# One attention and feed-forward layer on one core: projections, attention and feed-forward as three phases, key tiles in a new order over eight banks

## The chip, the core and the metric

The kernel runs on one core of one Trainium2 chip (trn2). The metric is the device time of one execution in microseconds (us), the median of several runs. "Before" is the kernel as it stands, "after" the changed one.

## What is computed

The input x has 4 batches of 512 tokens with 512 features, all in float32. Attention has 32 query heads of width 16 in 8 groups; each group of four query heads shares one key head and one value head. Then follows a layer norm of x plus the result, a sparse feed-forward step (in each block of 32 of its 1792 inner features one is kept, the one where a low-rank guess is largest), and a layer norm again.

```python
x = L0_attn_x
x = _layernorm(x + _L0_attn_ref(x, L0_attn_wq, L0_attn_wk, L0_attn_wv, L0_attn_wo), axis=-1)
x = _layernorm(x + _L0_ffn_ref(x, L0_ffn_c1_w, L0_ffn_c2_w, L0_ffn_w1, L0_ffn_w2t), axis=-1)
# attention, for every batch b and group g of NKV = 8:
scores = jnp.einsum('bqgrd,bkgd->bgrqk', qg, k) / jnp.sqrt(jnp.asarray(HD, x.dtype))
attn = jax.nn.softmax(scores.astype(jnp.float32), axis=-1).astype(x.dtype)
out = jnp.einsum('bgrqk,bkgd->bqgrd', attn, v)
```

## The kernel before

Where float32 accuracy is wanted from the faster matmul type, a tensor is held as a high part and a low part (`_h`, `_l`), and a product is three matmuls: high by high, high by low, low by high. A **unit** is one batch and one group: four query heads by 512 queries by 512 keys. There are NU = 32 units, in order of batch. A **key tile** is a quarter of a unit: 128 keys against all 4 x 512 queries.

*Projections.* `project(b, s)` (12 matmuls, L645) makes 128 rows of q, k or v of a batch; there are TASKS = 6 of them per batch. ScalarE copies the high part out of PSUM, VectorE the low part, and SyncE (`store_projection`, L202) writes both to DRAM (`q_stacks`, `k_stacks`, `v_halves`), from where `load_unit` (four transfers, L218 and L219) and `load_v` read them back. Batches 0 to 2 are projected ahead of attention; the six tasks of batch 3 lie between key tiles of the first units (`LATE_AT`).

*Attention.* The operands of a unit lie twice in SBUF, in rows 0 to 49 and 64 to 113, so a matmul uses the upper (a = 0) or lower (a = 1) half of TensorE's rows. For a key tile TensorE does:
- four **scores** `scores_t(n, kt, r)` (L707), keys by queries, each into one bank of `ps_st` (two banks), which ScalarE turns into `probs` by one exponential each (L486);
- one **weighted sum** `weigh` (L721), four heads side by side in 32 columns each, eight matmul records;
- four **maxima matmuls** `scores(n + 2, ...)` (L670), queries by keys, for the unit after next, whose rows VectorE reduces to maxima (L509) two at a time.

The maxima of a unit are subtracted inside the score matmul, as two more rows of q (the **shift**). Its way: VectorE splits them into high and low (L516, L518), TensorE turns them (`turn_max`, L689, four matmuls into bank `ps_x`), ScalarE copies them (L446), and SyncE sends them to rows 48, 49, 112 and 113 of q (L233). `scores_t` of the first key tile of a unit waits for `shift_in`. Once in a unit ScalarE moves the sums out (`take_sums`, L452). The output projection of a batch (`project_out`, L737, four of 12 matmuls), its residual and its layer norm lie in units 5 and 6 of the next batch; before it the sums are read back (`load_sums`), multiplied with reciprocals (L412, GpSimd) that one transfer has spread over partitions (L259), and split (L458 ScalarE in the key tiles of `HIGH_AT`, L415 GpSimd).

*Feed-forward.* 4 x 14 slots (b, m); in each TensorE does 12 matmuls up (L1211), one for the marks (L1222), 12 down (L1234) and four small transposes (L1199), with preparing steps (`slot_steps`) in between. Batch 3's output projection is a step there (`wo`, L1171), batch 0's first transposes and its low-rank product were done in attention (`turn_x`, `first_u`).

The order on each engine is written out by hand: each engine runs its own loop, and semaphores tie them. PSUM in attention: four banks `ps_max`, two `ps_st`, one `ps_pv`, one `ps_x`.

## Time and profile before

| | us |
|---|---|
| median of 3 runs (lowest, highest) | 1001.59 (998.66, 1003.35) |
| the profiled execution, its own time | 998.58 |
| its span, first to last instruction | 996.8 |
| TensorE busy | 908.2 (91%) |
| VectorE busy | 562.4 (56%) |
| ScalarE busy | 442.9 (44%) |
| GpSimd busy | 193.1 (19%) |
| mean granted TensorE clock, share of full | 0.944 |

"Busy" is the time in which an engine has an instruction in flight. TensorE's instructions overlap one another, so its share says little of how much work it does in that time. A row of the timeline or of a group gives the engine, the line of the kernel, the operation, what it writes and reads, and in square brackets how long the engine had stood idle and for whom it waited. "PEclk" is the granted clock as a share of 2.4 GHz: 1.00 is 2.4 GHz, 0.50 is 1.2 GHz.

### The profile page before, as it was taken

Reading aid. Unit: us, or ns where it says so; the run is one execution under the profiler, and the core shown is the slowest. Engines: PE = TensorE matmul, PEld = TensorE weight load, DVE = VectorE, ACT = ScalarE, POOL = GpSimd, SP = SyncE. Lnnn points to the kernel's source line nnn. Section 1 sums busy time; section 2 is a strip of 40 time slices with the busy share of each in tenths; the row PEclk is TensorE's granted clock in tenths of the full one; section 3 lists DMA queues with packets and bytes.
Section 4 is the critical chain, followed back from the end, with each engine's and each line's share of the span. In section 5 each row is a group of like instructions: output and inputs, shape, how many; then the busy total and the mean of one; then the engine's idle time right before and its main releaser. Section 6 shows DMA issues by size and latency. Waiting matters only on the chain. (4 is left out here: it accounts for less than half of the span.)

```text
span 996.8 us, 12134 instructions
## 1 busy us (share of the span) xinstructions
PE 908.2 (91%) x4472; PEld 533.0 (53%) x4472; DVE 562.4 (56%) x743; ACT 442.9 (44%) x821; POOL 193.1 (19%) x183
## 2 busy tenths in 40 slices
PE   5868999999899998999989975999999999999995
PEld 3745543333334333343333434777777777777774
DVE  4636567888656885468866533545563365326413
ACT  3302466777654775456765542322222222222231
POOL 6302003730210002100021002333321222122221
PEclk8889999999989998599988978999999999999998
DMA  8466535643342243323433124214030002001101
GB/s 249 160 205 240 169 110 159 175 123 91 91 117 69 76 134 80 97 85 79 135 82 109 34 97 102 82 44 155 14 116 11 1 3 103 2 1 43 42 1 42
DMA packets 50858, 92.99 MB, mean 93 GB/s; under 512 B 5648, under 2 KB 13840, under 8 KB 50288
## 3 DMA queue, kind: packets, MB, share of 16 engines
q1 hardware_dynamic: 49312, 87.05, 29.3%
q0 software_dynamic: 1488, 5.16, 1.9%
q8 instruction: 36, 0.59, 0.2%
q14 instruction: 22, 0.18, 0.1%
HBM read 56.80 MB, written 34.87 MB: 92 GB/s over the span
## 5 line engine op out<-in xcount | busy, mean ns | idle before, releaser
L509 DVE TENSOR_REDUCE neg_max<-ps_max 128x2 f32<-128x1024 f32 x256 | 302.9, 1217 | 90.1 <-PE ps_max L670 89.7
L486 ACT ACTIVATE probs<-ps_st 128x512 f32<-128x512 f32 x496 | 270.2, 595 | 142.6 <-PE ps_st L707 139.7
L707 PE MATMUL ps_st<-q,k 50*128 50x512 f32 x496 | 181.9, 511 | 28.5 <-ACT probs L486 27.6
L707 PEld LDWEIGHTS ps_st<-q,k 50*128 50x128 f32 x496 | 71.9, 192 | 203.1 <-ACT probs L486 156.8
L670 PE MATMUL ps_max<-k,q 48*128 48x512 f32 x512 | 152.8, 452 | 14.0 <-DVE neg_max L509 9.2
L721 PE MATMUL ps_pv<-probs,v 128*32 128x512 f32 x1024 | 147.3, 649 | 5.9 <-ACT probs L486 2.3
L978 POOL TENSOR_TENSOR g_l<-picked,g_h 128x512 fp32r<-128x512 f32 x56 | 73.1, 1306 | 286.9 <-ACT g_h L1017 286.9
L1003 ACT ACTIVATE mask_t<-ps_t 128x512 bf16<-128x512 bf16 x56 | 33.4, 597 | 163.6 <-PE ps_t L1199 163.6
L1211 PE MATMUL ps_h<-xt_h,w_h 128*128 128x512 f32 x224 | 93.8, 419 | 8.0 <-ACT relu L1010 8.0
L1073 DVE TENSOR_REDUCE top<-ps_prep 128x14 f32<-128x448 f32 x62 | 38.6, 623 | 99.0 <-PE ps_prep L1188 98.8
L670 PEld LDWEIGHTS ps_max<-k,q 48*128 48x128 f32 x512 | 75.6, 199 | 28.9 <-DVE neg_max L509 13.5
L1090 DVE SCALAR_TENSOR_TENSOR picked<-ps_z,relu 128x512 f32<-128x512 f32 x56 | 38.7, 691 | 90.6 <-ACT relu L1010 90.6
L1211 PE MATMUL ps_h<-xt_h,w_l 128*128 128x512 f32 x224 | 88.8, 397 | 0.0
L1211 PE MATMUL ps_h<-xt_l,w_h 128*128 128x512 f32 x224 | 88.8, 397 | 0.0
L1010 ACT ACTIVATE relu<-ps_h 128x512 f32<-128x512 f32 x56 | 33.6, 599 | 102.2 <-PE ps_h L1211 102.2
L1234 PE MATMUL ps_out<-w_h,g_h 128*128 128x512 f32 x160 | 71.2, 445 | 0.0
L1234 PE MATMUL ps_out<-w_h,g_l 128*128 128x512 f32 x160 | 63.2, 395 | 0.0
L1234 PE MATMUL ps_out<-w_l,g_h 128*128 128x512 f32 x160 | 63.0, 394 | 0.0
L1211 PEld LDWEIGHTS ps_h<-xt_h,w_h 128*128 128x128 f32 x224 | 43.1, 192 | 15.5 <-ACT relu L1010 8.1
L412 POOL TENSOR_TENSOR att<-att,inv 128x512 f32<-128x512 f32 x12 | 14.8, 1270 | 172.4 <-DMA inv<-reciprocals 172.4
L1211 PEld LDWEIGHTS ps_h<-xt_h,w_l 128*128 128x128 f32 x224 | 42.7, 191 | 9.4
L1211 PEld LDWEIGHTS ps_h<-xt_l,w_h 128*128 128x128 f32 x224 | 43.2, 193 | 6.2
(159 smaller groups left out, 1141.2 us busy)
## 6 DMA issues: line engine op xcount, KB each, us to landing
q_stacks<-parts SPq DMA_DIRECT2D x48, 256.0 KB
q<-q_stacks SPq DMA_DIRECT2D x64, 192.0 KB, 3.6
sums<-stage SPq DMA_DIRECT2D x32, 256.0 KB, 3.4
k<-k_stacks SPq DMA_DIRECT2D x64, 96.0 KB, 3.1
x_raw<-xT SPq DMA_DIRECT2D x16, 256.0 KB, 8.5
yf<-after_attention SPq DMA_DIRECT2D x4, 1024.0 KB, 5.3
w_raw<-w POOLq DMA_DIRECT2D x16, 224.0 KB, 3.1
w_raw<-w SPq DMA_DIRECT2D x14, 256.0 KB, 2.9
```

The lines of the kernel that those rows point to most:

```text
L486: nc.scalar.activation(probs[kt % 2][:, r], score_bank(n, r), ACT.Exp, scale=float(HD) ** -0.5).then_inc(exp_done, 1)
L509: nc.vector.tensor_reduce(neg_max[n % 2][:, i // 2, :, i % 2], ps_max[i % 2][:], AX.X, ALU.max, negate=True).then_inc(max_red, 1)
L670: mm = nc.tensor.matmul(ps_max[i % 2][:, a], q[n % QR][64 * a:64 * a + STACK, j, t * P:(t + 1) * P], k_[n % QR][64 * a:64 * a + STACK, :], ...
L707: nc.tensor.matmul(score_bank(n, r), k_[n % QR][64 * a:64 * a + ROWS, kt * P:(kt + 1) * P], q[n % QR][64 * a:64 * a + ROWS, j, :], start=T ...
L721: last = nc.tensor.matmul(ps_pv[32 * r:32 * r + VW], v[f % 2][:, kt, g], probs[kt % 2][:, r], start=(kt == 0), stop=(kt == TT - 1))
L978: nc.gpsimd.tensor_tensor(g_l[m % 2][:], picked[m % 2][:], g_h[m % 2][:].bitcast(F32), ALU.subtract).then_inc(g_ready, 1)
L1003: nc.scalar.activation(mask_t[m % 2][:], ps_t[:], ACT.Copy).then_inc(mask_t_ready, 1)
L1010: nc.scalar.activation(act_r[m % 2][:], ps_h[:], ACT.Relu).then_inc(relu_ready, 1)
L1073: nc.vector.tensor_reduce(top[t % 2][:], src, AX.X, ALU.max).then_inc(prep_half, 1)
L1090: nc.vector.scalar_tensor_tensor(picked[m % 2][:], ps_z[:], 1.0, act_r[m % 2][:], ALU.is_equal, ALU.mult).then_inc(picked_ready, 1)
L1211: last = nc.tensor.matmul(ps_h[:], w[:, k, m * P:(m + 1) * P], xx[b % 2][:, k], start=(k == 0 and n == 0), stop=(k == KT - 1 and n == 2))
L1234: last = nc.tensor.matmul(ps_out[t][:], g[m % 2][:, t * P:(t + 1) * P], w2_tile(*w, m), start=(m == 0 and n == 0), stop=(m == MT - 1 and n ...
```

## The change

- **Three phases.** All 24 projection tasks run first, the last two batches with the maxima of units 0 and 1 between them. q and k of all batches stay in SBUF (`parts`, four buffers laid over memory that is used later), v too; nothing of them goes to DRAM. `load_unit` copies a unit from SBUF to SBUF in 12 transfers.
- **Attention alone.** No projection and no output projection lies between key tiles. Bank `ps_x` becomes a third bank of `ps_st`, so all eight banks serve attention. A score waits until the third last exponential is done, not the second last.
- **New order of a key tile**: one maxima matmul, three scores, the weighted sum of the tile before, a score, three maxima matmuls, so that the row halves alternate. `take_sums` moves on ScalarE ahead of the third exponential of a unit's first key tile.
- **The shift goes another way.** VectorE turns the maxima itself (`nc.vector.transpose`, L498), GpSimd's queue writes them to DRAM in four transfers (L291), waits for these, and reads them back into q in two (L297). GpSimd's other work (`load_raw`, `high_raw`, `low_raw`, `scale`, `low_att`, `split_w1`) stands behind these sends in its one queue.
- **A front of the feed-forward phase** does the output projections of all four batches (16 x 12 matmuls, now into the banks of `ps_out`), with residual and norm, and batch 0's preparing steps. Batch 0's sums are scaled and split during attention (units 11 to 14), those of batches 1 to 3 in the front: `load_att(b)` reads the sums and spreads the reciprocals, GpSimd multiplies, ScalarE and VectorE split.
- In the slots `relu` writes into `picked`, and `pick` works in place; w2 is loaded from slot to slot into a buffer of its own.

**TensorE, one key tile in the middle of a unit** (`ps_st` scores, `ps_max` maxima, `ps_pv` weighted sum; `exp_done` counts exponentials, `max_red` reductions). Before:

```order
L707 MATMUL ps_st<-q,k 128x512 [waits exp_done]
L670 MATMUL ps_max<-k,q 128x512 [waits max_red]
L707 MATMUL ps_st<-q,k 128x512 [waits exp_done]
L670 MATMUL ps_max<-k,q 128x512
L670 MATMUL ps_max<-k,q 128x512 [waits max_red]
L707 MATMUL ps_st<-q,k 128x512 [waits exp_done]
L670 MATMUL ps_max<-k,q 128x512
L707 MATMUL ps_st<-q,k 128x512 [waits exp_done]
L721 MATMUL ps_pv<-probs,v 32x512 [waits stage_ready,exp_done]
L721 MATMUL ps_pv<-probs,v 32x512 x3
```

After:

```order
L602 MATMUL ps_st<-q,k 128x512 [waits exp_done] x3
L616 MATMUL ps_pv<-probs,v 32x512 [waits exp_done]
L616 MATMUL ps_pv<-probs,v 32x512 x3
L602 MATMUL ps_st<-q,k 128x512 [waits exp_done]
L589 MATMUL ps_max<-k,q 128x512 [waits max_red]
L589 MATMUL ps_max<-k,q 128x512
L589 MATMUL ps_max<-k,q 128x512 [waits max_red]
L589 MATMUL ps_max<-k,q 128x512
```

Of the four scores two stood ahead of the weighted sum and two behind, each next to a maxima matmul; now three stand ahead of it and one behind, and the maxima follow in one run.

**GpSimd, units 3 to 5 of the changed kernel** (`maxima` is the DRAM buffer of the shift, `max_rows` the turned maxima; `max_turned` counts turned units, `max_out` landed writes). The change's rows from the second transfer of one shift into q to the next shift's:

```order
L291 DMA maxima<-max_rows 4x8x32 x3
L297 DMA q<-maxima 2x1024 [waits st_mm,max_out]
L297 DMA q<-maxima 2x1024
L321 TENSOR_TENSOR wo_l<-wo_raw,wo_h 128x2048 [waits pre]
L322 TENSOR_TENSOR c_l<-c_raw,c_h 128x320
L324 TENSOR_TENSOR c_s<-c_raw,c_s 16x1792 [waits pre]
L291 DMA maxima<-max_rows 4x8x32 [waits max_turned,pre]
L291 DMA maxima<-max_rows 4x8x32 x3
L297 DMA q<-maxima 2x1024 [waits st_mm,max_out]
```

The splitting of wo, c1 and c2 (L321, L322, L324) stands between two shifts; the next shift's transfers can't be issued until it is done.

The diff, cut to its core:

```diff
@@ -59,281 +56,204 @@
...
-        ps_st = [ps(f"ps_st{j}", [P, S]) for j in range(2)]
+        ps_st = [ps(f"ps_st{j}", [P, S]) for j in range(3)]
         ps_pv = ps("ps_pv", [P, S])
-        ps_x = ps("ps_x", [P, S])
...
             def load_unit(n):
 
-                j, b = n % QR, n // NKV
+                j, b, g = n % QR, n // NKV, n % NKV
                 if n >= QR:
-                    sp.wait_ge(pv_done, TT * (n - QR + 1))
+                    sp.wait_ge(st_mm, TILES * (n - QR + 1))
                 elif n == 0:
-                    sp.wait_ge(ones_set, 2 * QR + 1)
-                if n % NKV == 0:
-                    for i in range(3):
-                        sp.wait_ge(part_out[i], DMA * parts_out((b + 1) * (REP + 1), i))
-                q_src = qs[n * Q_UNIT:(n + 1) * Q_UNIT].rearrange("(a p w) -> a p w", a=2, p=STACK)
-                k_src = ks[n * K_UNIT:(n + 1) * K_UNIT].rearrange("(p t) -> p t", p=STACK)
+                    sp.wait_ge(ones_set, 2 * QR)
+                if g == 0:
+                    sp.wait_ge(low_out, (REP + 1) * (b + 1))
+                src = parts[b][HD * g:HD * (g + 1)].bitcast(F32)
                 for a in range(2):
-                    rows = slice(64 * a, 64 * a + STACK)
-                    sp.dma_start(k_[j][rows].bitcast(F32), k_src).then_inc(unit_in[j], DMA)
-                    sp.dma_start(q[j][rows].rearrange("p j t -> p (j t)").bitcast(F32), q_src[a]).then_inc(unit_in[j], DMA)
-
-            def send_shift(n):
-
-                sp.wait_ge(shift_ready, n + 1)
-                for a in range(2):
-                    sp.dma_start(q[n % QR][64 * a + SHIFT:64 * a + SHIFT + 2].bitcast(F32),
-                                 shift[n % 2][4 * a:4 * a + 4].bitcast(F32)
-                                 ).then_inc(shift_in[n % QR], DMA)
+                    for c in range(3):
+                        rows = slice(64 * a + HD * c, 64 * a + HD * (c + 1))
+                        sp.dma_start(k_[j][rows].bitcast(F32), src[:, 0, (0, 0, 1)[c]]).then_inc(unit_in[j], DMA)
+                        sp.dma_start(q[j][rows].bitcast(F32), src[:, 1 + a::2, (0, 1, 0)[c]]).then_inc(unit_in[j], DMA)
...
@@ -358,92 +278,129 @@
...
+            def send_shift(n):
+
+                to = maxima[n * TILES * 2 * P:(n + 1) * TILES * 2 * P]
+                pool.wait_ge(max_turned, n + 1)
+                dst = to.rearrange("(c t o x) -> o t c x", c=8, t=TT, o=4)
+                for o in range(4):
+                    pool.dma_start(dst[o], max_rows[32 * o:32 * (o + 1)]).then_inc(max_out, DMA)
+                pool.wait_ge(max_out, 4 * DMA * (n + 1))
+                src = to.rearrange("(a h w) -> a h w", a=2, h=2)
+                if n >= QR:
+                    pool.wait_ge(st_mm, TILES * (n - QR + 1))
+                for a in range(2):
+                    pool.dma_start(q[n % QR][64 * a + SHIFT:64 * a + SHIFT + 2].rearrange("p j t -> p (j t)").bitcast(F32),
+                                   src[a]).then_inc(shift_in[n % QR], DMA)
...
+            send_shift(0)
+            for n in range(NU):
+                if n + 1 < NU:
+                    send_shift(n + 1)
+                if n == 1:
+                    load_raw()
+                if n == 3:
+                    high_raw()
+                if n == 4:
+                    low_raw()
+                if n == 12:
+                    scale()
+                if n == 14:
+                    low_att()
+                for i in range(KT * NC):
+                    if 22 + i // 2 == n:
+                        split_w1(i)
...
@@ -451,199 +408,162 @@
...
             for n in range(NU):
-                b, g = n // NKV, n % NKV
                 for kt in range(TT):
                     for r in range(REP):
                         i = (n * TT + kt) * REP + r
-                        if r == 2 and not b and (g, kt) in LATE_AT[1:]:
-                            high_projection(NB - 1, LATE_AT.index((g, kt)))
+                        if r == 2 and kt == 0 and n:
+                            take_sums(n - 1)
+                        if r == 3 and (n, kt) in HIGH_AT:
+                            high_att(HIGH_AT[n, kt])
                         act.wait_ge(st_mm, i + 1)
                         if r == 0 and n * TT + kt >= 2:
                             act.wait_ge(pv_done, n * TT + kt - 1)
-                        nc.scalar.activation(probs[kt % 2][:, r], score_bank(n, r), ACT.Exp,
+                        nc.scalar.activation(probs[kt % 2][:, r], ps_st[i % 3][:], ACT.Exp,
                                              scale=float(HD) ** -0.5).then_inc(exp_done, 1)
-                        if b and r == 2 and (g, kt) in HIGH_AT:
-                            high_att(b - 1, HIGH_AT.index((g, kt)))
-                    if kt == 0:
-                        if n:
-                            take_sums(n - 1)
-                    if kt == 1 and n + 1 < NU:
-                        turn_shift(n + 1)
             take_sums(NU - 1)
...
+            def turn_max(n):
+                dve.wait_ge(max_split, n + 1)
+                if n:
+                    dve.wait_ge(max_out, 4 * DMA * n)
+                nc.vector.transpose(max_rows[:], max_parts[:].rearrange("p t a h j -> p (t a h j)").bitcast(F32)
+                                    ).then_inc(max_turned, 1)
...
+                for kt in range(TT):
+                    step = n * TT + kt
+                    for pair in range(2 * step + TILES, 2 * step + 2 + TILES):
+                        if pair < NT // 2:
+                            row_max(pair)
+                        if n + 1 < NU and kt < 2:
+                            (high_max, low_max, turn_max, lambda n: None)[2 * kt + pair % 2](n + 1)
+                    if kt == 1 and n in DEN_AT:
+                        invert(DEN_AT[n])
...
@@ -651,167 +571,88 @@
...
             def scores_t(n, kt, r):
 
                 i = (n * TT + kt) * REP + r
                 if kt == 0 and r == 0:
                     pe.wait_ge(shift_in[n % QR], 2 * DMA * (n // QR + 1))
-                if i < 2:
-                    pe.wait_ge(evacuated, FRONT - 2 + i)
-                elif n < NU - 2 or (n, kt) == (NU - 2, 0):
-                    pe.wait_ge(exp_done, i - 1)
-                    if r == 2 and n == NU - 2:
-                        pe.wait_ge(max_red, 8 * NU)
+                if i < 3:
+                    task_taken(pe, max(j for j in range(LAST) if j % 4 == i))
                 else:
-                    pe.wait_ge(exp_done, i - 3)
+                    pe.wait_ge(exp_done, i - 2)
                 a, j = r % 2, r // 2
-                nc.tensor.matmul(score_bank(n, r), k_[n % QR][64 * a:64 * a + ROWS, kt * P:(kt + 1) * P],
+                nc.tensor.matmul(ps_st[i % 3][:], k_[n % QR][64 * a:64 * a + ROWS, kt * P:(kt + 1) * P],
                                  q[n % QR][64 * a:64 * a + ROWS, j, :], start=True, stop=True).then_inc(st_mm, 1)
...
+            for o in range(TASKS):
+                project(0, o)
+            for b in range(1, NB):
+                for o in range(TASKS):
+                    project(b, o)
+                    if o == 0:
+                        turn_v(b - 1)
+                    for pair in pairs_at(b, o):
+                        scores(2 * pair)
+                        scores(2 * pair + 1)
+            turn_v(NB - 1)
+            scores(2 * TILES)
             for n in range(NU):
-                b, g = n // NKV, n % NKV
                 for kt in range(TT):
+                    step = n * TT + kt
+                    ahead = 4 * step + 2 * TILES + 1
+                    scores(ahead)
                     scores_t(n, kt, 0)
-                    if n == 0 and kt == 0:
-                        scores(2, 0, 0)
-                    scores(n + 2, 2 * kt, 1)
                     scores_t(n, kt, 1)
-                    if kt or n:
-                        weigh(*divmod(n * TT + kt - 1, TT))
-                    if not b and (g, kt - 1) == LATE_AT[0]:
-                        turn_v(NB - 1)
-                    if not b and (g, kt) in LATE_AT:
-                        pe.wait_ge(shift_ready, n + 1 + (kt > 1))
-                        project(NB - 1, LATE_AT.index((g, kt)))
-                    if b and (g, kt) in WO_AT and n < NU - 2:
-                        project_out(b - 1, WO_AT.index((g, kt)), n + 1 + (kt > 1))
                     scores_t(n, kt, 2)
-                    scores(n + 2, 2 * kt + 1, 0)
+                    if step:
+                        weigh(*divmod(step - 1, TT))
                     scores_t(n, kt, 3)
-                    scores(n + 2, 2 * kt + 1, 1)
-                    scores(*divmod(8 * (n + 2) + 2 * kt + 2, 8), 0)
-                    if n == NU - 2 and (g, kt) in WO_AT:
-                        project_out(b - 1, WO_AT.index((g, kt)), n + 1 + (kt > 1))
-                    if n == NU - 2:
-                        turn_x(kt)
-                    if (n, kt) == (NU - 1, 1):
-                        first_u()
-                    if kt == 1 and n + 1 < NU:
-                        turn_max(n + 1)
+                    scores(ahead + 1)
+                    scores(ahead + 2)
+                    scores(ahead + 3)
             weigh(NU - 1, TT - 1)
...
+            def load_att(b):
+
+                if b >= 2:
+                    sp.wait_ge(att_split, REP * (b - 1))
+                src = sums[b * NKV * SUMS:(b + 1) * NKV * SUMS].rearrange(
+                    "(g r h d t) -> r h g d t", r=REP, g=NKV, h=2, d=HD)
+                for r in range(REP):
+                    sp.dma_start(att[:, r], src[r, 0]).then_inc(att_in, DMA)
+                if b == NB - 1:
+                    sp.wait_ge(rden_out, DMA)
+                at = b * NH * S
+                sp.dma_start(inv[:].rearrange("p r t -> p (r t)"),
+                             rden[at:at + NH * S].rearrange("(g o t) -> g o t", g=NKV, o=1).broadcast_to(
+                                 [NKV, HD, REP * S])).then_inc(inv_in, DMA)
...
+            def scale(b):
+                pool.wait_ge(att_in, REP * DMA * b)
+                pool.wait_ge(inv_in, DMA * b)
+                for r in range(REP):
+                    nc.gpsimd.tensor_tensor(att[:, r], att[:, r], inv[:, r], ALU.mult).then_inc(att_scaled, 1)
+
             pool.wait_ge(half_set, 1)
             low_w2(0)
+            scale(1)
+            root(0)
+            scale(2)
+            root(1)
+            scale(3)
+            root(2)
+            root(3)
...
+                project_out(0, t)
+            project_out(1, 0)
+            project_out(1, 1)
+            front(0)
+            front(1)
+            project_out(1, 2)
+            front(2)
+            front(3)
+            project_out(1, 3)
+            front(U)
+            project_out(2, 0)
+            front(marks(0, 0))
+            front(marks(0, 1))
+            project_out(2, 1)
+            front(marks(0, 2))
+            front(marks(0, 3))
+            project_out(2, 2)
+            project_out(2, 3)
+            inner_up(0, 0, (0, 1, 2, 3))
             turn_mask(0, 0)
+            for t in range(TT):
+                project_out(3, t)
```

## Rows read from the trace of the kernel before

**Rows 1.** Stages: stretch, length, busy of PE PEld DVE ACT POOL, clock, DMA share, GB/s
```profile
0.00:103.53 103.53, 75.12 (x277) 54.35 (x277) 51.60 (x63) 24.73 (x42) 28.17 (x32) 0.87 0.66 213
103.53:592.93 489.40, 450.32 (x2377) 184.50 (x2376) 330.08 (x372) 312.62 (x593) 69.16 (x76) 0.93 0.38 104
592.93:617.50 24.57, 14.49 (x58) 10.43 (x59) 9.99 (x16) 4.52 (x9) 3.90 (x4) 0.85 0.49 134
617.50:983.20 365.70, 365.26 (x1750) 281.58 (x1750) 163.18 (x275) 101.03 (x178) 90.83 (x71) 0.99 0.13 42
```

**Rows 2.** Page, costliest groups: busy, mean ns of one, idle before, what ended it
```profile
L509 DVE TENSOR_REDUCE neg_max<-ps_max 128x2 f32<-128x1024 f32 x256 | 302.9, 1217 | 90.1 <-PE ps_max L670 89.7
```

**Rows 3.** Timeline of one steady key tile: start us, length us, engine, line
```profile
350.81 0.51 PE L707 MATMUL ps_st<-q,k 50*128 50x512 f32 x2
...
351.35 1.09 ACT L486 ACTIVATE probs<-ps_st 128x512 f32<-128x512 f32 x2 [0.83 <-PE ps_st L707]
...
352.49 0.49 PE L707 MATMUL ps_st<-q,k 50*128 50x512 f32 x1
...
352.91 1.07 PE L721 MATMUL ps_pv<-probs,v 128*32 128x512 f32 x8
...
353.90 0.50 PE L707 MATMUL ps_st<-q,k 50*128 50x512 f32 x2
```

**Rows 4.** Timeline of VectorE, maxima split in two units that follow each other
```profile
353.90 0.17 DVE L516 CAST max_parts<-neg_max 128x16 fp32r<-128x16 f32 x1
...
366.41 0.17 DVE L516 CAST max_parts<-neg_max 128x16 fp32r<-128x16 f32 x1
```

**Rows 5.** Busy time by stretch: a wait, half clock, full clock, half clock again
```profile
265.80:268.97 3.17, 0.00 (x1) 0.01 (x1) 1.46 (x2) 1.17 (x3) 2.47 (x3) 1.00 0.31 111
269.50:283.50 14.00, 13.67 (x49) 4.47 (x48) 6.12 (x7) 8.02 (x15) 6.16 (x6) 0.51 0.23 61
284.00:300.00 16.00, 15.14 (x83) 6.51 (x80) 11.31 (x14) 9.74 (x20) 0.35 (x1) 1.00 0.49 131
390.00:418.00 28.00, 27.43 (x94) 9.21 (x95) 12.38 (x14) 14.71 (x28) 7.77 (x7) 0.50 0.24 66
```

**Rows 6.** Timeline of TensorE at half clock, the weighted sums of two tiles
```profile
406.64 1.93 PE L721 MATMUL ps_pv<-probs,v 128*32 128x512 f32 x8
...
411.19 1.93 PE L721 MATMUL ps_pv<-probs,v 128*32 128x512 f32 x8
```

**Rows 7.** Line L395, transfers issued by GpSimd: ns of an issue, us to landing
```profile
L395 POOL DMA_DIRECT2D w_raw<-w x16: 543/556/570, 161.2 to 206.5; - x16
...
DMA to landing us min/median/max: 2.7/3.1/5.1
```

**Rows 8.** DMA issues: KB each, median us from issue to landing
```profile
reciprocals<-inv_den SPq DMA_DIRECT2D x3, 64.0 KB, 1.6
```

**Rows 9.** Line L218, loads of k issued by SyncE: ns of an issue, us to landing
```profile
L218 SPq DMA_DIRECT2D k<-k_stacks x64: 307/422/1384, 53.1 to 526.1; - x64
...
DMA to landing us min/median/max: 2.0/3.1/8.4
```

**Rows 10.** Groups of instructions of the whole run, by line
```profile
L412 POOL TENSOR_TENSOR att<-att,inv 128x512 f32<-128x512 f32 x12 | 14.8, 1270 | 172.4 <-DMA inv<-reciprocals 172.4
...
L375 POOL TENSOR_TENSOR wo_l<-wo_raw,wo_h 128x2048 fp32r<-128x2048 f32 x1 | 4.6, 4552 | 0.1
```

**Rows 11.** Timeline of TensorE: the first matmul of the run
```profile
6.05 0.76 PE L645 MATMUL ps_st<-x_h,w_h 128*128 128x512 f32 x1 [6.05 <-DVE x_l L501]
```

**Rows 12.** Chain that ended last, two steps of it: start us, length us, what
```profile
603.95 12.36 DMA w_raw<-w
...
636.66 2.73 PE ps_prep L1171 x12
```

**Rows 13.** Timeline: reciprocals of batch 0 spread, and who waits for them
```profile
253.62 0.65 SPq L259 DMA_DIRECT2D inv<-reciprocals  x1
...
266.50 2.49 POOL L412 TENSOR_TENSOR att<-att,inv 128x512 f32<-128x512 f32 x2 [54.91 <-DMA inv<-reciprocals]
```

1037 lines of the change are left out of this document (454 added, 583 removed).

## Prediction

> **What bounds the kernel now.** I read the stages first, since one average would mix limits. By the busy times per stretch [rows 1], attention takes 489.4 us of the 996.8 us span and TensorE is busy in 450 of them; the slots of the feed-forward phase take 365.7 us with TensorE busy throughout; projections take 103.5 us with 28 us of TensorE idle. Then the costliest groups: VectorE's reductions of maxima are 302.9 us and stand idle 90 us for TensorE [rows 2], so VectorE does not bound attention, yet it puts a floor of 2.4 us under a key tile (two reductions).
>
> Third, the timeline of a steady tile [rows 3]. Scores at 350.81, exponentials from 351.35 (0.54 later), two of them in 1.09 us, ending 352.44; the next score at 352.49 (0.05 later); the weighted sum at 352.91 (0.42); the scores behind it at 353.90 (0.99). A tile is 3.09 us, and a unit without other work 12.51 us, by VectorE's split in two units [rows 4]. The tile is a loop: a score waits for an exponential to free one of two banks, the exponential for a score. TensorE's own work is shorter: at half clock, where it is 98% busy [rows 5], two weighted sums are 4.55 us apart [rows 6], so 2.3 us at full clock.
>
> Fourth, the clock. After TensorE idled 3.2 us at 265.8 the granted clock stood at 0.51 (1.2 GHz) for the next 14 us and came back to 1.00 with nothing but key tiles and the turning of the maxima on TensorE; a later one stayed at 0.50 for the 28 us shown [rows 5]. At half clock a tile is 4.55 us.
>
> **The change part by part.**
>
> *Projections.* Six tasks come forward from attention. A task is 12 matmuls of 128x512, 2.73 us by a step of the same shape in the chain [rows 12]. 24 of them are 65.5; the 33 maxima matmuls between them, at 2.73 / 12 = 0.23 each, 7.5; the first matmul starts at 6.05 [rows 11]; I add 5 for half clock at the start and for one late weight load. No q or k goes to DRAM and back. Sum 84 us, against 103.5 for 18 tasks, whose idle time the readback made.
>
> *A key tile.* I follow the new order round. The last exponential of a tile frees the bank of the third score: 0.05 later it runs, 0.42 later the weighted sum, 0.99 later the fourth score, 0.54 later its exponential, which takes 0.55. That is 2.55 us, all terms from [rows 3]. TensorE's 2.3 us and VectorE's 2.4 stay just under it. A unit's first tile costs more, since `take_sums` (one copy on ScalarE, about an exponential's length) stands before the third exponential and waits for the weighted sum: 3.2 us. Unit: 3 x 2.55 + 3.2 = 10.85 us, against 12.51. If the new run of three maxima lost the overlap of row halves, eight matmuls at 0.23 and 0.99 would make the tile 2.83 and the unit 12.0; that is the bound above.
>
> *The shift.* Here the change adds a wait. VectorE turns the maxima in a unit's second tile, by my count 5.2 us after the unit's first score (3.2 for the first tile, a reduction of 1.2 by [rows 2], 0.8 for the turn). From there GpSimd issues four transfers, waits for landing, and issues two more; the next unit's first score waits for these. The trace has no such way through this queue. Nearest are GpSimd's loads: 0.556 us an issue, 2.7 to 5.1 to landing, median 3.1, but of 224 KB each [rows 7]. These here carry 8 KB in all. Small writes of SyncE land in 1.6 us [rows 8], its loads in 2.0 at least [rows 9]. I take three issues (1.7), 2.0 for the write, one issue (0.55), 2.2 for the read and 0.2 for semaphores: L = 6.6 us, since the size is nearer to the small transfers. Ends: 5.9 with the fastest landings, 8.6 with 3.1 twice. The unit is then 5.2 + 6.6 = 11.8 us, not 10.85, and TensorE idles 0.95 us in each; by the ends 11.1 and 13.8. The four turning matmuls and ScalarE's copy vanish, off this path. The Trainium skill, page "DMA: Bandwidth & Descriptors", section "Anatomy of one DMA", gives a transfer of GpSimd about 2 us fixed and little for bytes; by it L would be some 6.4, while the trace's own rows of that queue say 8.6.
>
> At unit 4 the splitting of wo and c stands ahead of a shift in the queue: 4.55 us for wo [rows 10] and some 5 for c by size. That makes one shift about 2 us late, an idle time of some 3 us, which in the trace is what lowers the clock [rows 5]. I price one fall: 14 us at 4.55 instead of 3.1 us a tile loses 14 x (1 - 3.1 / 4.55) = 4.5 us.
>
> *Attention in all:* 32 x 11.8 = 378, plus 2 for the late shift, 4.5 for the fall and 3 for the last weighted sum: 387 us, against 489.4.
>
> *The front.* What stood in attention's gaps now stands alone. Batches 1 to 3 go through one `att` buffer, in rounds: sums read (4), reciprocals spread, product on GpSimd, split (2). The spread takes 12.9 us from issue at 253.62 to the multiplication that waited for it [rows 13]; the product is 4 x 1.27 [rows 10]. A round is 24 us. The first is about 10 longer, because w2's low part stands ahead of `scale(1)` on GpSimd. After the third come four output projection steps of 2.73 and what feeds the first slot, 13. So 34 + 24 + 24 + 13 = 95 us. TensorE has 16 x 2.73 = 44 us of work in it. Before, this stretch was 24.6 us [rows 1], with a 12.36 us load of w1 queued behind the spread on the chain [rows 12]. The front costs 70 more.
>
> *The slots.* The four output projection steps, 2.73 each [rows 12], leave: -10.9. Slot 1 enters them: +6.3 (twelve matmuls up and twelve down at 0.23, and small ones). 365.7 - 4.6 = 361. The w2 loads are covered, since the DMA share there is 0.13 [rows 1]. The end stays 13.6 (from 983.2 to the span's end).
>
> **Sum:** 84 + 387 + 95 + 361 + 13.6 = 940.6 us of span, against 996.8. The profiled execution took 1.8 more than its span, and the median of the runs is 3 above that execution: forecast 945 us.
>
> **The rivals.**
>
> *The shift is hidden.* For it: landings of 1.6 and 2.0 [rows 8, 9]. Against: GpSimd's rows [rows 7]. Units at 10.85 and no fall: -31 - 6, so 908 us.
>
> *Slower: the shift cools TensorE in every unit.* For it: landings near 5 occur in GpSimd's queue [rows 7], and if `L` reaches 8.8, TensorE idles 5.2 + 8.8 - 10.85 = 3.2 us in each unit, the length after which the clock fell [rows 5]. At half clock a unit is 4 x 4.55 = 18.2 us and the shift is in time; the clock returns after some 14 us, the next unit waits again, and so on in turn: about 15.3 us a unit, 32 x 3.5 = +112, or 1057 us. If it never returns, 32 x 6.4 = +205, or 1150. From a mean unit of 13.7 us on the change is slower, since 945 + 32 x 1.9 = 1006. Against: half the terms of L are issues, which vary by 5%, and so small a transfer has no reason to take the 3.1 us of 224 KB. The Trainium skill, page "TensorE: Matmul & The Clock Gate", section "HAM oscillation — how this bites in real kernels", tells of a kernel whose waits for transfers cool TensorE again in every round; that is this rival's mechanism, and by it the time would be the 1057.
>
> *The unit loads become the limit.* Twelve transfers, each from and to 16 partitions, replace four. Their issue at 0.42 is 5.0 us and landing is 2.0 to 8.4 [rows 9]; they start with the unit and the maxima need them some 10 us later. At the median 3.1 they are in time by 2 us; at 7 they cost 2 us in each unit, +64: 1009 us.
>
> *The front goes otherwise.* If the spread waits for nothing else, rounds are 5 shorter and it comes to 80; if half clock covers TensorE's work in it, to 115: 930 to 965 us.
>
> **How the numbers follow.** A measurement here tells 0.5% from no change. My forecast with its own bounds (unit 11.1 to 12.4, front 80 to 115) has 0.50, 915 to 985 us; the hidden shift 0.20, 890 to 915; the unit loads or a long L without a fall 0.15, 985 to 1020, a third of it above 1006; repeated falls 0.10; the change doing less than it says, with other waits between 997 and 1006, 0.05. The range of 890 to 1010 leaves out little more than the falls. Faster 0.80, same 0.05, slower 0.15.
>
> **What would show it.** The first score should start near 84 us; scores that begin a unit should lie 11.8 us apart and wait for the transfer into q; GpSimd's transfers should show landings near 2 us; the clock row should be at 9 or above, with one dip near unit 6; the first slot should end about 95 us after the last key tile. If the unit distance is over 13.7 us, or the clock row shows 5 to 7 through attention, the sign is wrong. If the distance is below 11, the shift was hidden.

## The result and the profile after

| | before | after |
|---|---|---|
| median, us (lowest, highest) | 1002.16 (998.66, 1003.35) | 1036.11 (1034.57, 1042.52) |
| the profiled execution, its own time | 998.58 | 1042.52 |
| span of the profiled execution | 996.8 | 1040.8 |

The changed kernel is slower: ratio 1.036, 95% interval 1.031 to 1.041. The forecast was 945 us, range 890 to 1010. Medians are of all executions, ratios only of those within 1.5% of a kernel's fastest, so the two differ where executions scatter (e3, e6, e8, e10).

Busy tenths and granted clock of the kernel after, in 40 slices of 26 us:

```profile
PE   7989988987799789898888356899999999999996
...
PEclk9989868788698977888876688899999999999998
```

Its stages; columns are stretch, length, busy time of PE, PEld, DVE, ACT, POOL, then clock, DMA share, GB/s. They answer to [rows 1]:

```profile
core 0: us, PE busy (x) PEld busy (x) DVE busy (x) ACT busy (x) POOL busy (x), PEclk, DMA share, GB/s
0.00:92.90 92.90, 81.76 (x339) 61.14 (x341) 52.16 (x73) 27.82 (x47) 7.83 (x22) 0.96 0.34 88
92.90:555.90 463.00, 406.01 (x2016) 148.43 (x2012) 305.11 (x337) 291.16 (x547) 174.43 (x257) 0.80 0.33 73
555.90:666.72 110.82, 64.53 (x248) 50.10 (x249) 52.46 (x99) 10.28 (x17) 21.02 (x18) 0.78 0.44 134
666.72:1027.30 360.58, 360.58 (x1733) 277.15 (x1732) 156.66 (x258) 101.35 (x178) 91.95 (x72) 1.00 0.13 41
```

| stage | forecast | measured | difference |
|---|---|---|---|
| projections | 84 | 92.9 | +9 |
| attention | 387 | 463.0 | +76 |
| front | 95 | 110.8 | +16 |
| slots | 361 | 360.6 | 0 |
| end | 13.6 | 13.5 | 0 |

Three quarters of the miss lie in attention, where the clock is 0.80: the clock row has 6 to 8 over most of it. A mean clock of 0.80 between levels 1.0 and 0.5 means 0.4 of the stretch, 185 us, at half clock (183 by the clock's own changes in the trace). I had allowed for 14.

The way of the shift that I had worked out is there, and nearly to size. The timeline of one unit (start us, us, engine, line):

```profile
340.41 0.73 PE L602 MATMUL ps_st<-q,k 50*128 50x512 f32 x3 [1.34 <-DMA q<-maxima]
...
344.25 1.06 PE L616 MATMUL ps_pv<-probs,v 128*32 128x512 f32 x8
...
345.19 0.20 DVE L498 STREAM_TRANSPOSE max_rows<-max_parts 128x32 f32<-128x32 f32 x1
...
345.68 2.43 POOL L291 DMA_DIRECT2D maxima<-max_rows  x4 [6.65 <-DVE max_rows L498]
...
346.85 0.16 PEld L616 LDWEIGHTS ps_pv<-probs,v 128*32 128x32 f32 x8 [0.24 <-issue]
...
349.45 0.16 PEld L616 LDWEIGHTS ps_pv<-probs,v 128*32 128x32 f32 x8 [0.24 <-issue]
...
349.53 1.07 POOL L297 DMA_DIRECT2D q<-maxima  x2 [1.42 <-DMA maxima<-max_rows]
...
352.28 0.29 PEld L602 LDWEIGHTS ps_st<-q,k 50*128 50x128 f32 x3 [0.98 <-DMA q<-maxima]
```

The first score is at 340.41. The maxima are turned at 345.19, 4.8 us later (forecast 5.2). The next unit's first score is at 352.28, 7.1 us after the turning (forecast 6.6), and the unit is 11.87 us (forecast 11.8). The two weighted sums in the middle are 2.60 apart (forecast 2.55). The first score waited for the transfer into q. GpSimd's two groups of transfers, ns of an issue and us to landing:

```profile
L291 POOL DMA_DIRECT2D maxima<-max_rows x128: 587/604/828, 75.2 to 529.5; - x128
...
DMA to landing us min/median/max: 1.7/2.0/6.7
```

```profile
L297 POOL DMA_DIRECT2D q<-maxima x64: 525/540/554, 79.2 to 532.0; - x64
...
DMA to landing us min/median/max: 1.8/1.9/7.6
```

The medians 2.0 and 1.9 are the small landings that I took (2.0, 2.2), not the 3.1 of [rows 7]; but the longest are 6.7 and 7.6. TensorE's 18 waits for the shift come to 32.5 us, where I had 0.95 in each of 32 units, 30. So the unit is right where the clock is 1.00; the next three readings show why it mostly is not.

**The clock falls after waits, short ones among them.** The wait at the head of another unit, and the clock around it in stretches:

```profile
221.66 0.73 PE L602 MATMUL ps_st<-q,k 50*128 50x512 f32 x3 [1.32 <-DMA q<-maxima]
```

```profile
221.00:222.50 1.50, 0.84 (x7) 0.45 (x11) 1.40 (x3) 0.30 (x1) 0.00 (x0) 1.00 0.41 78
222.50:224.00 1.50, 1.50 (x10) 0.50 (x4) 0.00 (x0) 1.19 (x3) 0.00 (x0) 0.70 0.38 68
224.00:229.00 5.00, 5.00 (x22) 2.10 (x19) 2.56 (x4) 3.11 (x7) 1.41 (x3) 0.50 0.48 94
230.00:232.00 2.00, 2.00 (x16) 0.75 (x15) 1.67 (x3) 1.58 (x4) 0.57 (x3) 1.00 0.04 5
```

TensorE had idled 1.32 us. From some 1.5 us after its return on, the clock is 0.50, until about 230. In the granted clock of the trace there are 16 falls in attention. Seven of them follow a single wait for the shift of 0.9 to 1.8 us; the clock was at half for 48 us after them. Eight follow waits of 3.1 to 7.5 us, four for the shift and four for VectorE's reductions; after them it was at half for 113 us. One, at 533.7, has no wait over 0.8 us near, and lasts through the remaining 22 us of attention. Three single waits of 1.05, 1.34 (the unit shown first) and 1.05 us, ended at 209.1, 340.4 and 468.5, were followed by no fall.

Two of the four long waits for the shift, one for the reductions:

```profile
133.98 1.22 PE L602 MATMUL ps_st<-q,k 50*128 50x512 f32 x3 [3.33 <-DMA q<-maxima]
...
272.71 1.22 PE L602 MATMUL ps_st<-q,k 50*128 50x512 f32 x3 [7.51 <-DMA q<-maxima]
...
248.13 0.80 PE L589 MATMUL ps_max<-k,q 48*128 48x512 f32 x2 [5.40 <-DVE neg_max L476]
```

The first two go with the longest landings above: the write landed late (6.7 us) after GpSimd had issued the loads of wo, c1 and c2, the read (7.6 us) while the 1 MB spread of batch 0's reciprocals was under way. That these transfers are the reason was tried only for the loads of a unit (e7, e9). The one at 441 stands behind the splitting of w1 in GpSimd's queue: the maxima are turned at 431.4 and their first transfer is issued at 434.3.

In the prediction I had only waits of 3.2 us to go by [rows 5]. The trace of the kernel before held shorter ones, at the end of attention, where I had not looked:

```profile
577.70 1.07 PE L721 MATMUL ps_pv<-probs,v 128*32 128x512 f32 x8 [1.52 <-ACT stage L452]
...
585.14 1.07 PE L721 MATMUL ps_pv<-probs,v 128*32 128x512 f32 x8 [0.92 <-ACT probs L486]
...
587.80 1.93 PE L721 MATMUL ps_pv<-probs,v 128*32 128x512 f32 x8 [1.17 <-ACT probs L486]
```

```profile
575.00:587.00 12.00, 9.19 (x58) 3.48 (x50) 3.68 (x8) 7.55 (x15) 1.01 (x1) 1.00 0.29 110
587.30:589.70 2.40, 1.90 (x8) 0.20 (x8) 0.00 (x0) 0.45 (x1) 0.00 (x0) 0.50 0.00 0
```

There the clock fell at 587.3 with no wait over 1.6 us in the 50 us before it.

**VectorE waits in three units for the denominators** (reciprocal L505 at 246.05, 4.66 us of idle) and so holds up the reductions and TensorE:

```profile
246.05 0.95 DVE L505 RECIPROCAL inv_den<-den 128x128 f32<-128x128 f32 x1 [4.66 <-DMA den<-sums]
```

**GpSimd's long subtractions hold up VectorE.** VectorE's two splits of the maxima, 0.17 us each elsewhere, and what GpSimd did meanwhile:

```profile
164.01 2.71 DVE L485 CAST max_parts<-neg_max 128x16 fp32r<-128x16 f32 x1
...
167.77 3.01 DVE L491 TENSOR_TENSOR max_parts<-neg_max,max_parts 128x16 fp32r<-128x16 f32 x1
```

```profile
161.30 4.56 POOL L321 TENSOR_TENSOR wo_l<-wo_raw,wo_h 128x2048 fp32r<-128x2048 f32 x1
...
166.75 3.99 POOL L324 TENSOR_TENSOR c_s<-c_raw,c_s 16x1792 fp32r<-16x1792 f32 x1
```

Each small operation ends when GpSimd's end: at 166.7 (the splitting of c1, 0.86 us, follows that of wo at once) and at 170.8. The reductions out of PSUM that run at the same time keep their 1.2 us. TensorE then waited 3.5 us for a reduction (at 172.0), and the half clock that followed lasted 24 us: this is the place for which I had priced my one fall of 14 us, reached through VectorE and not through the queue.

**The front** (steps of the chain of waits; start us, length us):

```profile
600.39 14.22 DMA inv_raw<-reciprocals
614.74 4.93 POOL att_raw L857 x4
```

The spread of the reciprocals takes 14.2 us (forecast 12.9), four products 4.9 (5.1). TensorE waits 17.9, 12.7 and 9.1 us for the three batches.

### The profile page after: what moved, and what is told of

Its sections match the earlier page's. It is cut to its first block and busy times, and to the rows that moved or that the text cites. A ratio compares the mean times of both kernels' runs of the same rounds, so it can differ in the third digit from the quotient of the medians.

```text
span 1040.8 us, 12101 instructions
## 1 busy us (share of the span) xinstructions
PE 916.0 (88%) x4344; PEld 539.0 (52%) x4344; DVE 574.0 (55%) x782; ACT 430.6 (41%) x789; POOL 296.7 (29%) x370
## 5 line engine op out<-in xcount | busy, mean ns | idle before, releaser
L444 ACT ACTIVATE probs<-ps_st 128x512 f32<-128x512 f32 x512 | 274.0, 601 | 150.9 <-PE ps_st L602 150.3
L602 PE MATMUL ps_st<-q,k 50*128 50x512 f32 x512 | 210.4, 536 | 38.7 <-DMA q<-maxima 32.5
L602 PEld LDWEIGHTS ps_st<-q,k 50*128 50x128 f32 x512 | 100.6, 224 | 229.1 <-ACT probs L444 148.8
L589 PE MATMUL ps_max<-k,q 48*128 48x512 f32 x512 | 157.4, 520 | 21.8 <-DVE neg_max L476 20.5
L616 PE MATMUL ps_pv<-probs,v 128*32 128x512 f32 x1024 | 171.4, 748 | 0.7 <-ACT probs L444 0.7
L291 POOL DMA_DIRECT2D maxima<-max_rows x128 | 77.8, 615 | 274.6 <-DVE max_rows L498 273.9
L962 DVE SCALAR_TENSOR_TENSOR picked<-ps_z,picked 128x512 f32<-128x512 f32 x56 | 38.7, 692 | 77.8 <-ACT picked L891 77.7
L891 ACT ACTIVATE picked<-ps_h 128x512 f32<-128x512 f32 x56 | 33.6, 600 | 105.6 <-PE ps_h L1125 105.6
L297 POOL DMA_DIRECT2D q<-maxima x64 | 34.2, 539 | 64.3 <-DMA maxima<-max_rows 64.3
```

The source lines that it names most:

```text
L291: pool.dma_start(dst[o], max_rows[32 * o:32 * (o + 1)]).then_inc(max_out, DMA)
L297: pool.dma_start(q[n % QR][64 * a + SHIFT:64 * a + SHIFT + 2].rearrange("p j t -> p (j t)").bitcast(F32), src[a]).then_inc(shift_in[n % QR ...
L444: nc.scalar.activation(probs[kt % 2][:, r], ps_st[i % 3][:], ACT.Exp, scale=float(HD) ** -0.5).then_inc(exp_done, 1)
L589: nc.tensor.matmul(ps_max[tile // 2 % 2][:, a], q[n % QR][64 * a:64 * a + STACK, j, t * P:(t + 1) * P], k_[n % QR][64 * a:64 * a + STACK, ...
L602: nc.tensor.matmul(ps_st[i % 3][:], k_[n % QR][64 * a:64 * a + ROWS, kt * P:(kt + 1) * P], q[n % QR][64 * a:64 * a + ROWS, j, :], start=Tr ...
L616: last = nc.tensor.matmul(ps_pv[32 * r:32 * r + VW], v[b][:, kt, g], probs[kt % 2][:, r], start=(kt == 0), stop=(kt == TT - 1))
```

## Experiments

Theory: the waits for the shift, through the clock, made attention long; the waits for the denominators and for VectorE beside GpSimd added to it. Rivals: the order of a tile, or the loads of a unit, set its length. All kernels were timed beside the kernel before; ratios are to it. "Attention" is from the first score to the end of the last weighted sum in each profile; a unit, in the stretches shown, is from one turning of the maxima on VectorE to the next. A profile is one execution, and may be far from the median.

**e1: the turning at the start of the unit.** All three operations need only maxima that were reduced in the unit before.

```diff
+                if n + 1 < NU:
+                    high_max(n + 1)
+                    low_max(n + 1)
+                    turn_max(n + 1)
                 for kt in range(TT):
...
-                        if n + 1 < NU and kt < 2:
-                            (high_max, low_max, turn_max, lambda n: None)[2 * kt + pair % 2](n + 1)
```

> The maxima of the next unit are split and turned at the very start of a unit, before its first reduction, not in its second key tile: the shift sets out some 3.5 us earlier, with the same transfers. If the wait of a unit's first score for the shift, and the fall of the clock some 2 us after such a wait, are what lengthened attention (mean unit 14.4 us, clock 0.82), most units come to 10.9 to 11.5 us at a clock of 1.00; the waits for the denominators (three) and the splitting of wo stay. Attention then goes from 463 to about 385 us and the whole to about 960 us. If instead the tile order or the loads of a unit set its length, the waits only change their name and the whole stays above 1020 us.

Measured: 995.9 us, ratio 0.985 (0.978 to 0.992). Attention, columns as above:

```profile
93.90:502.20 408.30, 358.15 (x2016) 133.75 (x2012) 304.61 (x337) 292.65 (x547) 174.88 (x257) 0.90 0.37 83
```

Against the changed kernel attention is 55 us shorter in the profiles, which are of executions of 1042.5 and 988.3 us; the medians are 40 us apart. TensorE's idle time fell by only 7 us (463.0 - 406.0 = 57.0, now 50.1); the other 48 us are busy time, 406 to 358, that is, the same matmuls at a higher clock. The falls went from 16 to 7, the time at half clock from 183 to 79 us, and the mean clock of a whole execution from 0.88 to 0.89 in four executions to 0.91 to 0.93 in four. The edit takes away both kinds of waits for the shift, the short ones and the long ones (1.2 us is the longest left), but not the waits for the denominators; and beside batch 0's spread a wait of 9.3 us for the operands stands where the shift had 7.5. Sixteen units came to 10.9 to 11.2 us. I had expected 385 us of attention and about 960 in all; 408 and 996 say that the waits left over weigh more.

**e2: the long waits taken away too.**

```diff
-                    if kt == 1 and n in DEN_AT:
-                        invert(DEN_AT[n])
+                    if kt == 0 and n - 1 in DEN_AT:
+                        invert(DEN_AT[n - 1])
...
+                if n == 5:
+                    low_c2()
```

(`low_c2` is the last operation of `low_raw`, L324.)

> As the run before, and VectorE inverts the denominators one unit later (unit 11, 19, 27), when they have long landed, and GpSimd splits wo and c1 in unit 4, c2 in unit 5. By the theory of waits and clock this takes away the three falls at about 243, 360 and 476 us and the one at 168 us, each 4 to 5 us of idle time and some 4 us at half clock: 25 to 35 us less than the run before, about 930 us. If these long waits were covered by something else, under 8 us.

Measured: 973.6 us, ratio 0.967 (0.959 to 0.975). Attention, one steady unit, and unit 14:

```profile
93.50:480.40 386.90, 351.31 (x2016) 129.91 (x2012) 302.02 (x337) 292.75 (x547) 174.46 (x257) 0.93 0.39 87
203.00:214.00 11.00, 10.53 (x68) 3.97 (x64) 9.85 (x11) 9.09 (x18) 3.50 (x6) 1.00 0.40 82
248.74:271.29 22.55, 16.68 (x77) 6.09 (x77) 10.08 (x11) 12.01 (x23) 9.47 (x12) 0.64 0.27 62
```

22 us less, of the 25 to 35 expected. The steady unit is 11.00 us (forecast floor 10.85). Unit 14 takes 22.6 us. TensorE's wait of 8.3 us for the operands (from 245.7 to 254.0) begins ahead of this stretch, and 5.3 us of it lie inside. The reading back of batch 0's sums and the spread stand ahead of these operands in SyncE's queue, so the rival about the loads is right in this place.

**e8: the late inversions and the parted splitting alone**, the turning left where the change has it: e2 without the edit of e1.

> The changed kernel with the late inversions and the parted splitting of e2, but the turning left in the second key tile. It takes away the long waits and keeps the short ones for the shift (0.9 to 1.6 us at the head of a unit). If short waits alone cool the clock, many units still show 0.8 to 0.9 and take 12.5 to 14 us, and the whole is 1005 to 1020 us. If the clock fell only after the long waits, units come to 11.9 us at a clock of 1.00 and the whole to about 985 us.

Measured: 1023.8 us, ratio 1.010 (1.003 to 1.017).

```profile
93.30:521.20 427.90, 375.59 (x2016) 136.26 (x2012) 303.15 (x337) 290.70 (x547) 174.42 (x257) 0.89 0.36 79
```

That is 4 us above the 1005 to 1020 that I expected if short waits alone cool the clock; the profiled execution took 1007.5. Beside e2 attention is 41 us longer in it. 17 us are idle time (52.3 against 35.6), 24 busy time at lower clock. The falls were 11 here and 5 in e2. Long waits were left, which the name of the run and my expectation leave out: five of the falls follow waits of 3.0 to 5.3 us for the shift, six a single one of 1.0 to 1.9 us. So it is these six that show that a short wait is enough, and not the whole time. And some waits left the clock alone: in units 7 to 11 waits of 1.76 and 1.37 us stand in stretches at 1.00. Idle time of a wait does not by itself decide.

**e4, e10, e12: order of the tile, and number of score banks.** e4 is e2 with the order of the kernel before; e10 is e4 with two banks; e12 is e2 with two banks.

```diff
                     ahead = 4 * step + 2 * TILES + 1
+                    scores_t(n, kt, 0)
                     scores(ahead)
-                    scores_t(n, kt, 0)
                     scores_t(n, kt, 1)
-                    scores_t(n, kt, 2)
                     if step:
                         weigh(*divmod(step - 1, TT))
+                    scores_t(n, kt, 2)
+                    scores(ahead + 1)
                     scores_t(n, kt, 3)
-                    scores(ahead + 1)
```

```diff
-                if i < 3:
+                if i < 2:
                     task_taken(pe, max(j for j in range(LAST) if j % 4 == i))
                 else:
-                    pe.wait_ge(exp_done, i - 2)
+                    pe.wait_ge(exp_done, i - 1)
...
-                nc.tensor.matmul(ps_st[i % 3][:]
+                nc.tensor.matmul(ps_st[i % 2][:]
```

> The second run's kernel with the key tile in the order of the kernel before (a score, a maximum, a score, the weighted sum, a score, a maximum, a score, two maxima). If the new order is what makes a tile 2.55 us, a tile here is near 3.1 us, a unit near 12.5 and the whole 40 to 55 us longer than the second run. If the third bank alone does it, the two are within 5 us.

> The kernel of e4 (tile order of the kernel before), and the scores use two banks in place of three, each waiting for the last but one exponential. If the third bank is what brought a unit from 12.5 to 10.9 us, units here take 12.3 to 12.6 us as in the kernel before, and the whole is 40 to 50 us above e4. If the loss of projections from between the tiles did it, units stay near 11 us.

> The kernel of e2 (new order of a tile), and the scores use two banks in place of three. With three scores in a row the third now waits for the tile's own first exponential. By the loop of waits a tile is then that exponential after the first score (0.54 + 0.55), the third score 0.05 later, the weighted sum 0.42, the fourth score 0.99, its exponential 0.54 + 0.55, the next tile's first or second score: 3.1 us, a unit 12.5 us, as in e10. If it is much longer than e10, the new order needs the third bank; if it is 11 us, the bank does nothing.

Measured: e4 971.4 us (0.964, 0.960 to 0.968); e10 1131.1 us (1.092, 1.088 to 1.097), its four runs from 1096 to 1168, where I had expected 40 to 50 us above e4; e12 1080.7 us, runs from 1059 to 1087, no interval. Attention and one unit of each, e4 first:

```profile
93.40:482.40 389.00, 351.38 (x2016) 120.62 (x2012) 303.45 (x337) 285.94 (x547) 174.47 (x257) 0.92 0.39 87
201.45:212.36 10.91, 10.42 (x68) 3.62 (x64) 9.87 (x11) 8.86 (x18) 3.50 (x6) 1.00 0.40 83
```

```profile
95.10:681.30 586.20, 578.37 (x2016) 201.19 (x2012) 302.20 (x337) 298.55 (x547) 174.92 (x257) 0.50 0.26 58
277.04:295.28 18.24, 18.24 (x68) 6.45 (x64) 9.96 (x11) 9.27 (x18) 3.51 (x6) 0.50 0.25 52
```

```profile
92.70:592.80 500.10, 465.88 (x2016) 156.31 (x2012) 302.29 (x337) 304.67 (x547) 174.40 (x257) 0.79 0.31 68
216.55:229.76 13.21, 12.26 (x68) 4.23 (x64) 9.96 (x11) 9.37 (x17) 3.49 (x6) 1.00 0.34 68
```

With three banks the old order gives 10.91 us a unit and the new one 11.00: the order is worth nothing. With two banks the new order takes 13.21 at full clock; I had expected 12.5, and the old order with two banks took 12.51 in the kernel before. What e10's unit would be at full clock can't be read: in its profile the clock fell in the first key tiles after the projections and stayed at 0.50 through the whole of attention, 586 us, with TensorE 99% busy. Its 18.24 us are four tiles of 4.56, as in [rows 6]. In e12 the clock fell seven times, six of them with no single wait over 0.7 us near, and stayed down for 58, 68 and 82 us in the longest. So the third bank pays in the tile. It seems to pay in the clock too, which came back after 3 to 17 us in e2; but in other profiles with three banks it stayed down for up to 34 us (e4, into the front) and 44 us (e3), so one profile of each kernel does not settle this.

**e3 and e5: w2 behind the first products of the front**, on the changed kernel and on e2.

```diff
+            scale(1)
             low_w2(0)
-            scale(1)
```

(and likewise `high_w2(0)` behind `high_att(1)`)

> The changed kernel, with one thing moved in the front of the feed-forward phase: the high and low part of the first block of w2 stand behind the first round of scaling on ScalarE and GpSimd, not ahead of it. In the trace w2 landed 20.9 us after its issue and the scaling of batch 1 began at 587.6. If the scaling waited for w2, it begins when the reciprocals have landed, 5 to 9 us earlier, and the whole is that much shorter (about 1029 us). If the spread of the reciprocals lands no earlier than w2, nothing changes.

> The kernel of e2 with the edit of e3 as well (w2 behind the first scaling in the front). If the two are independent, the gain of e3 stands here too: the first wait of the front (18.3 us in e2) shrinks by 5 to 10 us and the whole comes to 962 to 968 us. If e3's gain lay elsewhere, the first wait stays at 18 us.

Measured: e3 1021.5 us (1.009, 1.005 to 1.013), ten runs from 1010 to 1035; e5 968.4 us (0.964, 0.958 to 0.970). TensorE's first wait in the front, in e3 (the last number but the name):

```profile
578.31 0.76 PE L1103 MATMUL ps_out<-wo_h,att_h 128*128 128x512 f32 x1 [11.78 <-DVE att_l L968]
```

It was 17.86 us in the changed kernel; in e5 it is 13.52, in e2 18.30. So the edit is worth 5 to 6 us in the trace. e3 gained 15 us by medians of two series of runs. What it gained beyond these 5 to 6 us may be the scatter of the falls in attention; this was not shown. e5 against e2 is not resolved in time.

**e6: the spread in eight transfers** of 16 partitions, on e5.

```diff
+                for g in range(NKV):
+                    sp.dma_start(inv[HD * g:HD * (g + 1)].rearrange("p r t -> p (r t)"),
...
```

> As e5, and the reciprocals of a batch are spread by eight transfers of 16 partitions each (8 KB read per row of 16), in place of one transfer over 128 partitions that takes 13 to 14 us on the chain, against 5.3 us for another 1 MB transfer. If that one transfer is slow because of how it is cut (eight outer rows), it lands in 5 to 8 us after the last issue here, each of the three rounds of the front is 3 to 6 us shorter and the wait of 8.3 us in unit 14 shrinks: 10 to 25 us in all. If reading one row sixteen times is what is slow, nothing changes, or it gets longer by the seven more issues (4 us a round).

Measured: 977.5 us (0.964, 0.956 to 0.973). The spreads on the chain:

```profile
542.81 12.90 DMA inv_raw<-reciprocals
...
571.92 12.93 DMA inv_raw<-reciprocals
```

12.9 us, counted from the last of the eight issues. The first is 3.3 us earlier, so a spread takes 16.2 us from its first issue, where the one transfer took 14.2: nothing gained. Of two cuts neither is faster; what makes the transfer slow was not found.

**e7: wo loaded in four pieces**, in units 1 and 2, on e6.

```diff
+            def load_wo(r):
+                pool.dma_start(wo_raw[:, r], wo[r * P:(r + 1) * P]).then_inc(pre_in, DMA)
```

> As e6, and GpSimd loads wo in four transfers, two in unit 1, two with c1 and c2 in unit 2, in place of one of 1 MB in unit 1. In e2 the unit after these loads waits 1.7 us for its operands and 1.7 for its shift, and the clock falls: units 3 and 4 take 17.7 in place of 11. If the load of wo in one piece delays the small transfers, units 3 and 4 come to 11 to 13 us, 5 us less in all. If the many short rows of c1 do it, the wait moves one unit on and stays.

Measured: 972.0 us (0.967, 0.960 to 0.973). The two waits come 5 us later and are 1.6 and 1.4 us, after 2.6 and 1.2 in e6; units 4 and 5 together take 28.8 us, after 29.3. Nothing was gained that can be resolved.

**e9 and e11: batch 0's sums and reciprocals read back in four pieces**, one a unit, on e5; e11 with the old order as well.

```diff
-                if n == 11:
-                    load_att()
...
+                if 12 <= n < 12 + REP:
+                    load_att(n - 12)
```

> The kernel of e5, and in attention the sums and reciprocals of batch 0 are read back in four pieces of 256 KB each, one in each of units 12 to 15, with scaling and splitting moved to units 16 to 18, in place of all at once in unit 11. In e2 and e5 unit 14 takes 22.5 to 23 us and waits 8.2 us for its operands. If the large spread in front of the loads of a unit in the queue is the cause, all units from 12 to 18 take 11 to 12.5 us at a clock of 1.00: 10 to 14 us less than e5, about 956 us. If GpSimd's products in these units are the cause, the long unit moves to 17 and nothing is gained.

> The kernel of e9 with the tile order of the kernel before. By e4, whose units took 10.89 against 11.01 us, the whole should be 0 to 4 us under e9; it is to show that the order of a tile is worth nothing with three banks, at another point than e4 did.

Measured: e9 962.9 us (0.959, 0.955 to 0.963); e11 952.2 us (0.947, 0.941 to 0.952). Units 14 and 15 of e9, then attention and the same units of e11:

```profile
251.70:262.69 10.99, 9.22 (x57) 3.47 (x53) 9.86 (x11) 8.06 (x16) 3.51 (x6) 1.00 0.61 145
262.69:278.38 15.69, 15.64 (x75) 6.14 (x75) 9.97 (x11) 10.16 (x19) 3.51 (x6) 0.67 0.39 99
```

```profile
93.50:470.70 377.20, 344.33 (x2016) 119.10 (x2012) 303.43 (x337) 286.30 (x548) 174.53 (x257) 0.94 0.41 90
246.41:257.32 10.91, 10.43 (x68) 3.62 (x64) 9.87 (x11) 8.86 (x18) 3.50 (x6) 1.00 0.58 147
257.32:268.22 10.90, 10.40 (x68) 3.62 (x64) 9.87 (x12) 8.85 (x18) 3.49 (x6) 1.00 0.52 124
```

e9 is 6 us below e5, of the 10 to 14 expected. The 22.6 us of unit 14 are gone; in e9 one wait of 1.33 us still cooled the next unit to 15.7, in e11 none did. e11 is the fastest version: 5.3% below the kernel before, with everything of the change in it but the tile order, and five moves. That it beats e9 by 11 us is more than its tile, 0.1 us a unit, can give: in its profile the clock falls four times and not five, and for shorter.

## Why the prediction was wrong

- *The key tile and the unit at full clock:* right (2.60 and 11.87 us for 2.55 and 11.8; 11.00 for the floor of 10.85 in e2). That the order of the tile could lose the overlap did not come true; but I gave the gain to the order as much as to the bank, and e4 gives it to the bank alone; by e12 the order without the bank is 0.7 us a unit slower than the kernel before.
- *The shift:* right in its steps, in its usual length (7.1 for 6.6 us) and in the idle time that it costs by itself (32.5 for 30 us). Not right in its spread: landings of 6.7 and 7.6 us and work ahead of it in GpSimd's queue made four waits of 3.1 to 7.5 us, where I had put in one. The lower end of L is 6.1 us by its own terms, not 5.9. By the rule of the Trainium skill's page "DMA: Bandwidth & Descriptors", section "Anatomy of one DMA", on GpSimd's transfers, about 2 us fixed, the trace agrees in the median (2.0 and 1.9).
- *The clock:* the step that failed. "I price one fall", 14 us at half clock, worth 4.5 us: the runs show 16 falls and 183 us at half clock in attention. Two things were wrong in it. I counted one wait of some 3 us, and there were eight of 3.1 to 7.5 us, with 113 us at half clock after them. And "an idle time of some 3 us, which in the trace is what lowers the clock": seven falls, with 48 us, came after single waits of 0.9 to 1.8 us. I read the shortest wait before which I had seen a fall as the shortest that makes one, though [rows 5] held no wait between 1 and 3 us and the end of attention in the same trace did. So the 0.95 us of idle time that I put in each unit was priced at 0.95, and the rival of repeated falls was tied to L of 8.8 us in every unit and got 0.10. Its result, 1057 us, and its alternation of cooled and warm units are near what came: mean unit 14.5 us, for 15.3. The Trainium skill's page "TensorE: Matmul & The Clock Gate", section "HAM oscillation — how this bites in real kernels", describes the same cooling again and again by waits for transfers; the trace agrees in that, with 11 of its 16 falls behind waits for the shift.
- *Size of that step:* 185 us at half clock in place of 14. At 11.8 and 18.2 us a unit the 171 us more cost 171 x (1 - 11.8 / 18.2) = 60 of the 76 us, by estimate. That e1 moved only the shift's start and brought the time at half clock down to 79 us shows that the waits for the shift made the larger part of it.
- *Left out of the sum:* VectorE's wait for the denominators in three units (5.4, 3.9 and 3.5 us of TensorE), since I costed the inversions at nothing without asking when their load would land. In e2 they are gone, and GpSimd's hold on VectorE is down to one wait of 1.1 us of TensorE, for 22 us together.
- *The unit loads as the limit:* wrong as a limit of every unit (landings of 2.0 to 2.4 us in the median, though the twelve issues take 7.7 us and not 5.0), true in two places (in e2 units 4 and 14). In unit 14 a spread of 1 MB stands ahead in the queue, and cutting it up took the wait away (e9); in unit 4 the loads of wo and c are under way, and cutting wo up did not (e7).
- *Projections, +9:* TensorE is busy 81.8 us where I had 78, and idles 11, not 6.
- *The front, +16:* first round 35 us as forecast (34), the second 32.5 in place of 24, because SyncE waits for the last reciprocals (`inverted`), which VectorE makes behind batch 0's residual, and so issues `load_att(2)` only 7.1 us after the first round's end, and because GpSimd's root (1.0) and VectorE's norm (1.9) stand ahead of the split; the third 27, the end 16.5.
- *The slots and the end:* right to 1 us.

Open: why the clock stayed up after some waits of 1.3 to 1.8 us and fell after others of 0.9; why it fell near the end of attention with no such wait near; why two banks without work between the tiles kept it down for 586 us of attention, where the kernel before came back after 14 to 31.

## What to carry to other kernels

Read the clock as a cost that a wait can set off, and do not take the shortest wait seen before a fall for a bound: a new idle microsecond that recurs in each round of a loop should be priced at both clocks. And price a transfer on such a path with its longest landing as well as its median: here two landings of 6.7 and 7.6 us, beside medians of 2, stood before two falls of 20 us each. When a change puts a longer way (a transfer to DRAM and back) between a result and its user, first ask whether its start can move up; here that took no more than three operations moved by a few microseconds, and it turned 3.6% slower into 1.5% faster. When dense work goes from between short matmuls, look whether the clock still comes back: with two banks it did not (e10), for a reason that stays open.

## What the runs showed of the hardware that was not expected

- TensorE's clock fell to 0.50 after single idle times of 0.9 to 1.8 us, and six times in e12 with none over 0.7 us near. It stayed there for 3.4 to 30.7 us in the changed kernel, up to 82 us in e12 and for all 586 us of attention in e10, where TensorE was 99% busy.
- While GpSimd subtracts float32 tiles in SBUF (4.0 and 4.6 us), an operation of VectorE from SBUF to SBUF that takes 0.17 us took 2.7 and 3.0 and ended with GpSimd's; in e2 the same cast beside one of 0.86 us took 0.83. VectorE's reductions from PSUM kept their time.
- A spread of 64 KB over 128 partitions (1 MB written) takes 13.9 to 14.2 us in one transfer in the front, and 16.2 from the first issue in eight.
